# Swin block on one core: Q and K of the first band from three rounded products, and the first hidden chunk ahead of them

## The reference

```python
h = _ln(x, g1, b1)
h = jnp.roll(h, (-SS, -SS), axis=(1, 2))
xw = _win_part(h)                       # windows of 7 x 7 tokens
qkv = xw @ w_qkv + b_qkv
...
attn = jnp.einsum('whnd,whmd->whnm', q * HD ** (-0.5), k)
attn = attn + bias[None]
attn = attn.reshape(B, NW, NH, N, N) + MASK[None, :, None]
attn = jax.nn.softmax(attn.reshape(-1, NH, N, N), axis=-1)
out = jnp.einsum('whnm,whmd->whnd', attn, v)
out = out.transpose(0, 2, 1, 3).reshape(-1, N, C) @ w_proj + b_proj
...
x = shortcut + h
h2 = _ln(x, g2, b2)
h2 = jax.nn.gelu(h2 @ w_fc1 + b_fc1, approximate=False) @ w_fc2 + b_fc2
return x + h2
```

## Time and profile before

| | us |
|---|---|
| time, median of 3 runs | 3496.33 (3493.62 to 3499.7) |
| span of the profiled execution | 3490.6 |
| outside the span (median minus span) | 5.7 |
| PE busy | 3322.6 (95%) |
| PE weight loads busy | 2896.0 (83%) |
| DVE busy | 2984.1 (85%) |
| ACT busy | 2339.0 (67%) |
| POOL busy | 1302.4 (37%) |

### The profile page before, as it was taken

One profiled execution on the slowest core, in us unless ns is written; L12 is line 12 of the kernel. 1 busy time (PEld: TensorE's weight loads), 2 busy tenths in 40 slices (PEclk: granted clock), 3 DMA queues, 4 the chain that ended last, 5 costly groups with the idle time before them and its releaser, 6 DMA issues.

```text
span 3490.6 us, 89114 instructions
## 1 busy us (share of the span) xinstructions
PE 3322.6 (95%) x31504; PEld 2896.0 (83%) x31504; DVE 2984.1 (85%) x7836; ACT 2339.0 (67%) x5886; POOL 1302.4 (37%) x775
## 2 busy tenths in 40 slices
PE   5999999999999999999999999999999999999999
PEld 4888888888888888888888888888888888888887
DVE  7888888889888898888888888888889888898895
ACT  3667666666666676666766666666666666676665
POOL 2333333333333333333433333333334333343342
PEclk9999999999999999999999999999999999999999
DMA  2111111111111111111111111111111111111111
GB/s 60 43 48 47 48 44 48 46 50 43 48 46 50 44 47 46 50 43 43 50 50 44 43 49 50 45 45 46 46 50 43 48 46 49 44 49 46 49 37 30
DMA packets 261108, 161.88 MB, mean 46 GB/s; under 512 B 25914, under 2 KB 260506, under 8 KB 260634
## 3 DMA queue, kind: packets, MB, share of 16 engines
q1 hardware_dynamic: 260389, 155.39, 17.1%
q10 hardware_dynamic: 245, 0.04, 0.0%
HBM read 52.56 MB, written 51.38 MB: 30 GB/s over the span
## 4 chain that ended last, share of the span: by engine, by line
PE 76%; DVE 12%; ACT 6%; issue 6%; SPq 0%; DMA 0%; POOL 0%; DVEq 0%; ACTq 0%; POOLq 0%
PE psum L874 18%; PE psum L743 10%; PE psum L784 8%; PE psum L776 7%; PE psum L786 6%; PE psum L785 6%; PE psum L760 6%; PE psum L791 5%; PE psum L835 5%; PE psum L750 3%; PE psum L826 2%; ACT xT L444 2%; DVE scores L614 2%; DVE row_max L618 2%; ACT oT L434 2%
## 5 line engine op out<-in xcount | busy, mean ns | idle before, releaser
L874 PE MATMUL psum<-wfc,hT 128*112 128x128 f32 x7168 | 835.6, 274 | 1.0 <-ACT hT L480 0.7
L874 PEld LDWEIGHTS psum<-wfc,hT 128*112 128x112 f32 x7168 | 797.8, 177 | 38.9 <-issue 37.9
L368 POOL TENSOR_TENSOR probs<-probs,row_inv 128x784 f32<-128x784 f32 x256 | 389.2, 1520 | 1150.3 <-DVE row_inv L630 1150.3
L480 ACT ACTIVATE hT<-psum,bias_h 128x392 f32<-128x392 f32 x1024 | 583.1, 592 | 324.6 <-PE psum L786 324.1
L426 ACT ACTIVATE probsT<-psum 128x512 f32<-128x512 f32 x512 | 277.3, 596 | 412.3 <-PE psum L760 412.3
L602 DVE TENSOR_SCALAR xn<-x_in,mean,rstd 112x128 f32<-112x128 f32 x896 | 467.6, 588 | 38.9 <-POOL rstd L388 38.9
L743 PE MATMUL psum<-kd,qT 128*49 128x196 f32 x4096 | 413.5, 345 | 89.5 <-issue 86.2
L380 POOL TENSOR_TENSOR stream<-stream,brow_fc 112x896 f32<-112x896 f32 x128 | 268.4, 2097 | 487.6 <-DVE xn L602 487.6
L784 PE MATMUL psum<-x2T_hi,wfc_hi 128*128 128x392 f32 x1024 | 432.7, 423 | 2.3 <-DVE x2T_lo L655 2.1
L614 DVE TENSOR_TENSOR scores<-psum,bias_rel 128x784 f32<-128x784 f32 x256 | 249.0, 973 | 215.1 <-PE psum L743 215.0
L743 PEld LDWEIGHTS psum<-kd,qT 128*49 128x49 f32 x4096 | 251.9, 126 | 202.9 <-issue 115.3
(11 more groups left out here) (78 smaller groups left out, 6313.3 us busy)
## 6 DMA issues: line engine op xcount, KB each, us to landing
kd<-kT SPq DMA_DIRECT2D x1024, 49.0 KB, 2.0
x_in<-in_x SPq DMA_DIRECT2D x224, 196.0 KB
out<-stream SPq DMA_DIRECT2D x224, 196.0 KB
x_in<-in_x SPq DMA_DIRECT2D x32, 112.0 KB
out<-stream SPq DMA_DIRECT2D x32, 112.0 KB
x_in<-in_x SPq DMA_DIRECT2D x32, 84.0 KB
out<-stream SPq DMA_DIRECT2D x32, 84.0 KB
wfc_raw<-in_w_fc SPq DMA_DIRECT2D x1, 256.0 KB, 2.7
```

Source lines behind the costliest of these rows:

```text
L368: pool.tensor_tensor(p, p, r.unsqueeze(2).to_broadcast([128, PAIRS * HEADS, N]), ALU.mult).then_inc(probs_normed, 1)
L480: act.activation(hT[:, chunk, band * BAND:(band + 1) * BAND], tok_psum(FC1 + n)[:, 0:BAND], ACT.Gelu, bias=bias_h[:, chunk:chunk + 1]).the ...
L874: last = pe.matmul(tok_psum(FC2 + h)[0:TOK, (t - t0) * C:(t - t0 + 1) * C], hT[:, chunk, t * TOK:(t + 1) * TOK], wfc2[:, chunk, :], start= ...
```

## The change

`xT_hi` and `xT_lo` get a second half, for band 0. `round_x` and `split_x` take the band as an argument and are called for both. On ACT, `round_x(at, 0)` stands right behind the second half of `copy_x`, ahead of the table change. On DVE, `split_x(at, 0)` stands behind the first half of `split_x2` and ahead of `copy_v1`. On PE, `make_q` and `make_k` of band 0 use `product` like those of band 1, `make_q` waits for `xT_split` in place of `xT_copied`, and `make_hidden(at, 0)` stands ahead of `make_q(at, 0)` instead of between it and `make_k(at, 0)`. On ACT, `gelu(at, 0)` moves ahead of `copy_q(at, 0)` to follow that order.

```diff
-        xT_hi = sb("xT_hi", [C, BAND], F32R)
-        xT_lo = sb("xT_lo", [C, BAND], F32R)
+        xT_hi = sb("xT_hi", [C, BANDS, BAND], F32R)
+        xT_lo = sb("xT_lo", [C, BANDS, BAND], F32R)
...
                 if at.has(1):
                     copy_x(at, 1)
+                    round_x(at, 0)
                 if at.has(-1):
...
                     copy_x2(at, 1)
+                if at.has(-1):
+                    gelu(at, 0)
                 if at.has(1):
                     copy_q(at, 0)
-                if at.has(-1):
-                    gelu(at, 0)
-                if at.has(1):
                     copy_k(at, 0)
...
                 if at.has(1):
-                    round_x(at)
+                    round_x(at, 1)
...
                 if at.has(-1):
                     split_x2(at, 0)
+                if at.has(1):
+                    split_x(at, 0)
                 if at.has():
                     copy_v1(at)
...
                 if at.has(1):
-                    split_x(at)
+                    split_x(at, 1)
...
             def qk_product(at, use, part, band):
-                if band == 0:
-
-                    return pe.matmul(qkvo_psum(use)[:, 0:BAND], wqk[:, part, :], xT[:, at.slot(1) % 2, 0, :, 0:N],
-                                     start=True, stop=True)
                 return product(qkvo_psum(use)[:, 0:BAND], wqk_hi[:, part, :], wqk_lo[:, part, :],
-                               xT_hi[:, :], xT_lo[:, :])
+                               xT_hi[:, band, :], xT_lo[:, band, :])
 
             def make_q(at, band):
 
-                if band == 0:
-                    wait(pe, xT_copied, at.count(2, 2, 1))
-                else:
-                    wait(pe, xT_split, at.count(1, 1, 1))
+                wait(pe, xT_split, at.count(2, band + 1, 1))
...
+                if at.has(-1):
+                    make_hidden(at, 0)
                 if at.has(1):
                     make_q(at, 0)
-                if at.has(-1):
-                    make_hidden(at, 0)
-                if at.has(1):
                     make_k(at, 0)
```

More of the change, by code:

```diff
@@ L445, in copy_x, with round_x @@
                 last.then_inc(xT_copied, 1)
-            def round_x(at):
+            def round_x(at, band):
                 wait(act, xT_copied, at.count(2, 2, 1))
-                act.activation(xT_hi[:, :].rearrange("c (w n) -> c w n", n=N),
-                               xT[:, at.slot(1) % 2, 1, :, 0:N], ACT.Copy).then_inc(xT_rounded, 1)
+                act.activation(xT_hi[:, band, :].rearrange("c (w n) -> c w n", n=N),
+                               xT[:, at.slot(1) % 2, band, :, 0:N], ACT.Copy).then_inc(xT_rounded, 1)
             def copy_x2(at, h):
@@ L503, in step @@
                     copy_x2(at, 1)
-                if at.has(1):
-                    copy_q(at, 0)
                 if at.has(-1):
@@ L508, in step @@
                 if at.has(1):
+                    copy_q(at, 0)
                     copy_k(at, 0)
@@ L641, in copy_v1, with split_x @@
                 last.then_inc(v1_copied, 1)
[L643 to L648, removed]
+            def split_x(at, band):
+                wait(dve, xT_rounded, at.count(2, band + 1, 1))
+                dve.tensor_tensor(xT_lo[:, band, :].rearrange("c (w n) -> c w n", n=N),
+                                  xT[:, at.slot(1) % 2, band, :, 0:N],
+                                  xT_hi[:, band, :].rearrange("c (w n) -> c w n", n=N),
                                   ALU.subtract).then_inc(xT_split, 1)
@@ L918, in step @@
                     transpose_x2(at, 1)
-                if at.has(1):
-                    make_q(at, 0)
                 if at.has(-1):
@@ L923, in step @@
                 if at.has(1):
+                    make_q(at, 0)
                     make_k(at, 0)
```

## The result

The changed kernel took 3804.62 us (3798.68 to 3806.12, 4 runs) against 3498.01 us of the kernel before on the same chip: 1.087 times as long, with a 95% interval of 1.0855 to 1.0887. The forecast was 3618 us, 3.5% slower. The sign was right, the size was not: 307 us were lost where 122 had been worked out.

A forecast was written before the change was run, and what follows sets the result against it. K's tie to DVE's copies of V was taken to bound the kernel through L760's start. Three regular steps of 1.00 plus a first of 0.85 gave 121 us, with the run-in 122: 3618 us, range 3580 to 3650.

The forecast's parts named there:

- What bounds the kernel: K of band 0 starts when DVE's copies of V end; PE then runs solid, so L760's start moves the whole step.
- PE's saving of 0.36 us: PE from the end of the transposes to L760: 2.27 us without any wait instead of 2.63, at most 0.36 a step.
- The wait for ACT and the lateness of V: DVE ahead of V's copies: 0.49 us of work and 0.66 waiting for ACT's rounding, so V starts 1.15 us later.
- The sum's overlap of 0.08 us: DVE, new difference L646 (0.567 us) before V's copies: assumed instruction overlap of 0.08, so L640 starts 0.49 us after it.
- The price of the difference: DVE's split_x for band 0, ahead of the copies of V: one more L646, priced at 0.567 us.
- A wait of 1.0 us should leave the clock where it is: PE idles about 1.0 us in each step, before K; the granted clock was to stay at 2.4 GHz.
- The fourth rival: PE's idle 1.0 us brings the lower clock once a step: 1.3 us a step, 165 us, 3780 us; chance 4 in 100.
- The wait of 2.32 us: Earlier PE wait at 71.52, in a 178.7 us stretch at 2.4 GHz, cited for the clock holding.
- Nothing else late: ACT's probsT copies keep 0.26 us to spare, DVE still waits for scores, kd transfers stay hidden; worst allowed 0.25 a step.

The follow-up runs named there:

- PE's part alone: Kernel before with chunk 0 ahead of Q, band 0's Q and K from three products of feed-forward input parts, no new ACT or DVE work: 3494.78 us, 0.9994 times.
- the order alone: Kernel before with only hidden chunk 0 and its gelu moved ahead of Q of band 0, which stays one float32 product: 3496.7 us, 1.0001 times.
- Where nothing collides, the run: Changed kernel with GpSimd normalising only one of 16 rows of band 1 (L368 cut short): 3621.37 us, 1.036 times the kernel before.
- the two runs with filling: Changed kernel with three unread float32 products ahead of Q and three between Q and K of band 0: 3715.59 us; with those ahead of Q alone: 3709.81 us.

## Why the prediction was wrong

1. *What bounds the kernel.* Right. K's start is tied to V, and PE's saving of 0.36 us is worth nothing while DVE and ACT stay as they are: PE's part alone measured 0.9994, the order alone 1.0001.
2. *The wait for ACT and the lateness of V.* Right for what it counted. DVE waited 0.60 us for the rounding (0.6 forecast). Where nothing collides, the run took 3621 us, against 3618 forecast, and regular steps 0.96 us more, against 1.00. The last 4 us of that agreement may be luck: the clock was at its lower level 29 times there and 23 before, which the sum doesn't have. The sum's overlap of 0.08 us between the difference and the copies of V was not in its rows either, where L655 and L640 overlap by 0.03 (1709.74 + 0.62 - 1710.33); the run then showed 0.49 us from start to start (1768.58 to 1769.07), as assumed.
3. *The price of the difference.* **This is the step that failed.** It was taken as 0.567 us from the mean of L646 for band 1. That mean is of a place where GpSimd does only small work; the new place lies under L368. It took 1.22 us there, 0.65 more, and V was 1.8 us late instead of 1.15. The forecast looked at what DVE, ACT and PE do at the new time and not at what GpSimd does. A sign of it stood in the rows: seven L602 took 3.67 us in that step, while in the changed kernel the same seven instructions take 1.87 us where GpSimd has ended its long addition (at 1823.06, a step with the slow clock). The Trainium skill says it outright ("SBUF — State Buffer", section SBUF: two separate sides): a DVE instruction with two SBUF inputs and a GpSimd instruction that reads SBUF take turns on a shared pair of ports, each for its whole length. The trace agrees, with 1.22 us beside L368 and 0.57 without it. It doesn't agree for L388, on 7 columns, which also reads SBUF: the difference ran inside its 1.49 us and took its usual 0.57, so the measurement decides there, as far as the span recorded for GpSimd can be trusted.
4. *"A wait of 1.0 us should leave the clock where it is."* Right for one wait (of 1.17 or 1.38 us, 30 falls against 23 of before, none behind the wait within the loop), wrong for what came: the collision made two waits, 0.70 and 0.85 us in regular steps and 0.8 to 1.1 and 0.84 us in first ones. The fourth rival had the mechanism, with 4 in 100, but as a fall in every step; it fell in 36 more places, mostly first and second steps of an image, and cost about 90 us, the difference between the changed kernel and the two runs with filling. The wait of 2.32 us that the forecast leaned on the earlier trace rows left the clock up, so the length of the idle time alone doesn't decide it.
5. *Nothing else late.* Right for ACT and the scores in regular steps. Behind a fall of the clock the difference of band 1 was late too, and met L396: 43 times, with 42 us of waits on PE.

The account of the 307 us: 123 us for the later V as forecast (3621 - 3498), some 92 us more for the collision with the clock held (3710 or 3716 against 3621), and some 92 us for the clock (3805 against the same), in which the second collision's waits are counted. What stays open is why the clock falls in some steps with both waits and not in others with the same ones (13 of 31 second steps, 1 third, no fourth); no run here separates that.

## What to carry to other kernels

Before an instruction is priced from its mean elsewhere, look at what every engine does at the new place, GpSimd among them; a mean is also the mean of its surroundings. Where an engine that is nearly always busy waits briefly for the same partner once in every step, it is that partner's time that is for sale, and PE work saved ahead of the wait is worth nothing. Several new short waits close together have to be added up before one says that the clock will hold, and the worst step counts, not the regular one.

## What the runs showed of the hardware

- A DVE subtraction of two SBUF operands (392 columns) that starts under a GpSimd multiplication of 784 columns ends 0.41 to 0.43 us after it, whenever it started (127 steps of the changed kernel); the same holds under a GpSimd addition of 896 columns (43 times). Beside a GpSimd instruction on 7 columns it takes its usual 0.57 us, and a DVE subtraction with one operand in PSUM took its usual 0.62 us beside the multiplication.
- PE waits of 0.84, 1.17 or 1.68 us alone, once in a step, were not followed by the lower clock in any regular step of the loop. In all, 29 and 30 falls to 1.2 GHz in the trace went with the first two, 23 to 29 with kernels that have no such wait. A single wait of 2.0 to 2.1 us was followed by it in 15 of 22 steps; waits of 0.8 to 1.1 and 0.84 us with one product between them in 28 of the 30 first steps that had them; waits of 0.70 and 0.84 us in 13 of 31 second steps, 1 third and no fourth. Filling one of the two with work that nobody reads gave back 2.5%.
